# A GNN kernel's first message stage with TensorE's program as straight code instead of a loop over four groups

## What is computed

```python
Wxh = x @ Wl.T + bl
h = silu(rbf @ Wf1.T + bf1)            # rbf: 212,500 x 64
f_ij = h @ Wf2.T + bf2
msg = f_ij * Wxh[j]                    # j: destination nodes, sorted
agg = segment_sum(msg, i, 12500)       # i: source nodes
y = x + agg
```

## Time and profile before

| | |
|---|---|
| median of three runs | 4407.96 us |
| lowest, highest | 4403.15, 4412.23 us |
| time of the profiled execution | 4366.64 us |
| its span, first to last instruction | 4364.9 us |
| busy: TensorE matmul / weight load | 58% / 47% of the span |
| busy: VectorE / ScalarE / GpSimd | 62% / 20% / 55% |
| granted TensorE clock, mean | 0.73 |
| matmuls, weight loads | 28074, 28075 |
| packets of the queues of kind "instruction": q8, q14 | 89 (1.46 MB), 57 (0.47 MB) |

### The profile page before, as it was taken

How to read it: one execution, slowest core, us unless ns; L and a number is a source line. 1 busy time by engine, 2 the same in 40 slices (tenths; PEclk the granted TensorE clock), 3 DMA queues, 4 the chain that set the end, 5 groups by cost and what they waited for, 6 DMA issues and landing times. The chain is left out here.

```text
span 4364.9 us, 81175 instructions
## 1 busy us (share of the span) xinstructions
PE 2517.8 (58%) x28074; PEld 2052.6 (47%) x28075; DVE 2725.6 (62%) x5354; ACT 888.6 (20%) x1671; POOL 2381.8 (55%) x2228
## 2 busy tenths in 40 slices
PE   3565665555565565665555655555475166666775
PEld 3454444444444444444444444444464155555763
DVE  5555555555555555555555555555566899997776
ACT  2111111111111111111111111111111355551002
POOL 0466666566565665655656656656122655554452
PEclk9677777777677676767767777776798555558998
DMA  7422222222222222222222222221686199999992
GB/s 213 96 68 68 68 68 63 64 69 67 61 70 64 65 71 61 69 66 61 68 67 61 69 65 67 69 61 51 234 332 250 57 306 303 305 306 354 406 406 96
DMA packets 205906, 585.25 MB, mean 134 GB/s; under 512 B 57272, under 2 KB 74432, under 8 KB 193216
## 3 DMA queue, kind: packets, MB, share of 16 engines
q1 hardware_dynamic: 134016, 369.03, 27.5%
q0 software_dynamic: 68336, 213.37, 13.4%
q10 hardware_dynamic: 3408, 0.92, 0.1%
HBM read 389.22 MB, written 194.13 MB: 134 GB/s over the span
## 5 line engine op out<-in xcount | busy, mean ns | idle before, releaser
L1019 POOL DMA_INDIRECT region_rows<-x_space,pos x1664 | 1797.4, 1080 | 1128.2 <-DVE x_space L972 632.2
L972 DVE TENSOR_TENSOR x_space<-rest,x_space 128x512 bf16<-128x512 f32 x208 | 144.0, 692 | 1010.2 <-issue 628.0
L886 PEld LDWEIGHTS ps_fx<-tmp_space,window 128*128 128x128 bf16 x9984 | 483.1, 116 | 532.1 <-issue 528.7
L868 PE MATMUL ps_rank<-onehot,tri 128*128 128x98 bf16 x1664 | 160.2, 265 | 872.0 <-DVE onehot L907 866.9
L886 PE MATMUL ps_fx<-tmp_space,window 128*128 x9984 | 521.7, 218 | 241.5 <-issue 238.9
L868 PEld LDWEIGHTS ps_rank<-onehot,tri 128*128 128x128 bf16 x1664 | 118.6, 128 | 933.2 <-DVE onehot L907 927.6
L880 PE MATMUL ps_th<-in_t,w_wf 128*128 128x512 f32 x416 | 424.6, 1124 | 0.0
L823 ACT ACTIVATE hid_t<-ps_th,w_bf 128x512 f32<-128x512 f32 x208 | 143.0, 687 | 1162.4 <-remote 699.4
L894 PE MATMUL ps_fx<-w_wf,hid_t 128*128 128x128 f32 x1664 | 318.5, 342 | 40.2 <-issue 35.9
L894 PEld LDWEIGHTS ps_fx<-w_wf,hid_t 128*128 128x128 f32 x1664 | 268.6, 240 | 55.8 <-issue 55.2
L818 ACT COPY in_t<-ps_th 128x512 f32<-128x512 f32 x208 | 121.9, 586 | 767.5 <-PE ps_th L861 551.5
(11 more groups left out here) (232 smaller groups left out, 4776.5 us busy)
## 6 DMA issues: line engine op xcount, KB each, us to landing
tmp_space<-region_rows SPq DMA_DIRECT2D x98, 882.0 KB, 6.6
run_rows<-agg SPq DMA_DIRECT2D x98, 873.0 KB
x_space<-key_rows SPq DMA_DIRECT2D x98, 576.0 KB
x_space<-rbf SPq DMA_DIRECT2D x208, 256.0 KB
rel_bc<-rel_rows SPq DMA_DIRECT2D x208, 256.0 KB
region_rows<-x_space,pos POOLq DMA_INDIRECT x1664
region_rows<-x_space SPq DMA_DIRECT2D x1, 14259.0 KB, 73.5
wxh_rows<-agg POOLq DMA_DIRECT2D x1, 3328.0 KB, 23.3
```

What stands on the lines that cost most here:

```text
L868: e.matmul(ps_rank[:, 0:NB], tri[:, :], onehot[j % 2][:, t, :], start=(t == 0), stop=(t == T - 1))
L886: last = e.matmul(ps_x[:, t * D:(t + 1) * D], window_t[:, h, t * P:(t + 1) * P], wxh[:, bass.ds(b + h, 1), c, :].rearrange("p b d -> p (b ...
L1019: e.indirect_dma_start(out=region_rows, out_offset=bass.IndirectOffsetOnAxis(ap=pos[j][:, t:t + 1], axis=0), in_=rows_f[j][:, t, :], in_of ...
```

## The change

TensorE's hardware loop becomes a Python loop: the four-group body is emitted 52 times, with i a constant in each. The line-857 read of b takes a constant column. Nothing else is edited; b stays a register, and SyncE, ScalarE, VectorE and GpSimd keep their loops.

```diff
@@ -852,9 +852,9 @@
                 def _(e):
                     seed(e, rk, tr, h1, f2, xw)
                     e.matmul(ps_pairs[0:NB, 0:NBP], zeros[:, 0:NB], zeros[:, 0:NBP], start=True, stop=False).then_inc(f_zero, 1)
-                    with e.Fori(0, passes) as i:
+                    for i in range(passes):
                         for j in range(S):
-                            b = e.value_load(base_i[0:1, bass.ds(i * S + j, 1)], min_val=0, max_val=NB - 1)
+                            b = e.value_load(base_i[0:1, i * S + j:i * S + j + 1], min_val=0, max_val=NB - 1)
                             e.wait_ge(ld[j], i * 16 + 16)
                             e.wait_ge(ev, count_of(i, j, 1))
                             for t in range(T // 2):
```

## The result

The changed kernel takes 4662.06 us (median of four runs, 4637.69 to 4664.88) beside 4405.56 us for the kernel before (four runs, 4379.65 to 4412.23): ratio 1.058, 95% interval 1.053 to 1.064. It is 5.8% slower, where no change was forecast and 4480 us was the upper end of the range. That is the figure of one chip; on three others the changed kernel took 0.4 to 7.3% more than the kernel before, which is the harder half of this study.

A forecast was written before the change was run, and what follows sets the result against it. A ring of engine waits plus holds of TensorE's signals during GpSimd's scatters was taken to bound the stage. 4366.6 us profiled, minus 0, plus 0, with the 41.3 us offset carried, gave 4408 us; range 4340 to 4480.

The forecast's parts named there:

- the ring of 957, 907, 880, 823, 972: Chain of waits between engines, by source line, taken with the hold as the stage's period; turns of 12.30 and 14.23 us.
- the holds during bursts: While GpSimd issues scatters back to back, TensorE's signals get through late; 15 long waits at line 957, 151.7 us together.
- signs of being wrong: Matmul gaps between 868 and 880 near a q8 packet, a shrinking wait at 868, or long holds changing in number or length.
- The arriving code: Straight code must be fetched on q8, about 150 packets in the stage; bounded at 17 to 90 us, taken as nothing.
- The rival that requests for code are held: GpSimd's bursts delay packets missing between 868 and 880: 45 x 2.0 = 90 us, 4498 us; chance 0.15, small price 0.12.
- A gain of all 117 us: Upper end for removing TensorE's branch (10.8 us) and line 874's address arithmetic (106.5 us); lower end nothing, and nothing taken.
- The rest of i's arithmetic is a few instructions: Term for TensorE's other register arithmetic: a few instructions a group of 30 to 60 ns, within the some 117 us removed.
- Some 15 waits of 10 us at line 957, unmoved: Expected sign: VectorE's long holds stay as before, each after GpSimd's loss of 1.4 us.
- TensorE's signals fall earlier into GpSimd's bursts: Rival: leaner issue moves a quarter of the turns halfway, 50 us go, 4358 us; chance 0.15.
- small shifts may be enlarged: Argument for the earlier-signals rival: turn lengths jump between a few values, so a small shift could have a larger effect.

The follow-up runs named there:

- e7: Kernel before with TensorE's loop as two iterations of 104 written-out groups, line 874's register arithmetic kept: 0.999 of the kernel before.
- e11: The kernel of e7 (two written-out halves, line 874's arithmetic kept), measured again: 1.000 of the kernel before.
- e17: The kernel of e7 (two written-out halves, line 874's arithmetic kept), on another chip: 1.001 of the kernel before.
- e1: Kernel before with all 208 groups written out under a one-turn loop, folded at build, so the changed kernel's TensorE program plus three instructions ahead: 0.993 of the kernel before.
- e2: Kernel before with TensorE's loop as 13 iterations of 16 written-out groups, register arithmetic kept: 0.996 of the kernel before.
- e13: Changed kernel with the two waits ahead of line 868 (one-hot, counts) in the other order: 1.072 of the kernel before.
- e14: Kernel before with the two waits ahead of line 868 (one-hot, counts) in the other order: 1.002 of the kernel before.
- e8: Kernel before with TensorE's loop as 26 iterations of 8 written-out groups: 1.000 of the kernel before.

## Why the prediction was wrong

**What bounds the kernel** was read rightly: the ring of 957, 907, 880, 823, 972 and the holds during bursts. So was what the change does: 150 more packets on q8 were estimated and 149 came; no branch; the wait at 868 did not shrink. Of its signs of being wrong, the last came true: the long holds changed in number.

**The arriving code**, costed at nothing, cost nothing that could be found: e7, e11 and e17 bring as much and stand at 0.999 to 1.001, on chips that hold no signals. On B, which does, e1 and e2 bring it too and stand at 0.993 and 0.996. The rival that requests for code are held, 4498 us, got the sign and not the cause: TensorE's wait at 868 grew, and from 868 to the end of 880, where that rival put its cost, the changed kernel on A is not slower (3.82 us against 3.89).

**The step that failed** is the costing of what is removed: "A gain of all 117 us is the upper end, nothing the lower, and a removal cannot cost." It failed twice. The small part is in the term "The rest of i's arithmetic is a few instructions": taking the register out of line 866 moved the last wait to an instruction of its own, 208 x 0.09 = 19 us. The large part is the holds, 151.7 us at line 957, left unmoved in the sum ("Some 15 waits of 10 us at line 957, unmoved"). They became 628.9 us, and the steps between groups grew by 308 us, where the whole loss is 293 us.

**The rival** "TensorE's signals fall earlier into GpSimd's bursts" named the mechanism and its place, and had the wrong sign: it priced an earlier signal at a gain of 50 us. The gain was there at line 823, whose nameless wait fell from 699.4 to 160.5 us. On A and D it was more than lost behind it: the early signal fuses two bursts, and the later signals (886, 894, 861) find no pause for 20 us. Its remark that small shifts may be enlarged was the right one, and should have widened the range on both sides.

**What stays open.** That the large loss lies in held signals after fused bursts is what the traces on A and D account for (the steps between groups grew by 308 us, the profiled execution by 293); no run took that away on a chip where it was present. Why line 880's signal is not held in the written-out kernels on A and D is not shown: the place of the wait is ruled out (e13), written-out code that keeps the arithmetic at 874 ran only where no signals are held (e7, e11, e17), and the array's own times are nearly equal. On B the arithmetic does not decide it: e2 keeps all of it and its signal leaves early as well. Nor is the early signal enough: e1 and e2 on B have it (8.98 and 8.91 us, next scatters at 11.86 and 11.80), yet there the ring kept up after 70 of 101 and 48 of 82 fused steps, against 18 of 99, and they lost nothing. The changed kernel was not run on B, nor e1 on A or D. The twins agree on C, but C holds no signals, so whether B or the three instructions ahead of e1's program made it fast is not known.

## What to carry to other kernels

Where a ring of engines waits on signals that another engine's burst of scatters can hold, take no edit as free because it only removes work, and put both signs of the hold in the range. When a loop on an engine is written out, look in the trace at which instruction carries the wait that ends last ahead of its critical operation. The order in the source does not tell it: here, with constants, that wait had to stand first of the two to end up on the load itself (e13, 42 ns in place of 105). And repeat a comparison on a second chip before believing its size: the same pair of programs differed by 0.4% on one chip and by 7.3% on another.

## What the runs showed that was not expected

- The chips differ by more than the change. The kernel before takes 3898 us on two of them and 4348 to 4406 us on three, with the same instructions. What the traces show to differ is whether TensorE's signals get out while GpSimd issues scatters: line 880's leave within 0.01 us of its end on C and E and, in the median, 1.5 us after it in the kernel before on A. What makes one chip hold them and another not is not known.
- Held signals leave at a few moments of a burst, several at once: in the changed kernel on D, 874's leaves at 8.93 us of the burst, 1.9 us after its work ends, and 880's at 8.98 us; in e14 874's leaves at 9.66 and 880's at 9.71 us. These moments are not only the gaps between scatters: of the 175 signals of line 880 that left late in the kernel before, 79 left within the row of a scatter.
- TensorE's sequencer keeps a loop of eight groups at hand (e8, 92 packets in the whole span) and not one of 16 (e2, 14 packets an iteration, 3.7 us a branch). The Trainium skill, page "Runtime: NRT & Kernel Launch", section "Instruction fetch mechanics", gives TensorE room for 2048 instructions and brings them in blocks of 256. An estimate from it: e7's 248 - 89 = 159 packets for 208 groups are 196 instructions a group, 1,570 for eight and 3,130 for 16. The change of behaviour between the two agrees with that figure. By the same estimate 16 groups are 12 packets; why 14 came is open.
